# Second feed-forward in pairs of steps, its rank-2 additions in four groups of 32 rows, w13's low parts made by VectorE

## What is computed

```python
def attn(x, w_gate, w_up, w_down):           # I = 2752
    s = silu(x @ w_gate.T)
    s = s with its k = I/2 smallest |s| of each token set to 0
    return (s * (x @ w_up.T)) @ w_down.T

def qlora_linear(x, wq, A, B):               # wq is a quarter as wide; A, B have rank 2
    return x @ tile(wq, (1, 4)).T + (x @ A.T @ B.T) * 0.5

def ffn(x):
    return qlora(silu(qlora(x, w1q, a1, b1)) * qlora(x, w3q, a3, b3), w2q, a2, b2)

x = layernorm(x + attn(x)); x = layernorm(x + ffn(x))
```

## Time and profile before

| | us |
|---|---|
| median of 3 runs (2041.89 to 2043.99) | 2042.1 |
| the profiled execution's own time | 2044.99 |
| its span, first to last instruction | 2043.2 |
| PE busy in the span | 2001.4 |
| POOL busy | 1094.4 |
| DVE busy | 1110.7 |
| ACT busy | 799.2 |

### The profile page before, as it was taken

The page is one execution under the profiler, slowest core; times in us unless marked ns, Lnnn a source line. Parts: engine busy times, 40 slices in busy tenths (PEclk is TensorE's granted clock), DMA queues, the critical chain, the costliest instruction groups (busy, mean ns, idle before and its releaser), DMA issues.

```text
span 2043.2 us, 26001 instructions
## 1 busy us (share of the span) xinstructions
PE 2001.4 (98%) x9472; PEld 1635.8 (80%) x9472; DVE 1110.7 (54%) x1650; ACT 799.2 (39%) x1336; POOL 1094.4 (54%) x828
## 2 busy tenths in 40 slices
PE   8999999999999999999999999999979999999998
PEld 6887878888888888888888888887767777777776
DVE  0148984589763248976433888650145353454543
ACT  3357343562334347332333642422325325153251
POOL 6446984355546444644644455445738447175381
PEclk9999999999999999999999999999999999999999
DMA  4333333233434332433433243434422405124031
GB/s 139 97 92 86 116 102 92 83 114 118 135 88 126 97 94 93 139 119 104 125 97 94 93 138 96 133 94 154 137 78 93 144 21 174 42 90 146 21 133 42
DMA packets 104173, 213.40 MB, mean 104 GB/s; under 512 B 11896, under 2 KB 18040, under 8 KB 103012
## 3 DMA queue, kind: packets, MB, share of 16 engines
q1 hardware_dynamic: 99440, 194.97, 31.1%
q10 hardware_dynamic: 4608, 16.78, 2.1%
HBM read 194.93 MB, written 16.78 MB: 104 GB/s over the span
## 4 chain that ended last, share of the span: by engine, by line
PE 78%; issue 8%; POOL 8%; ACT 3%; DVE 2%; DMA 1%; SPq 0%; POOLq 0%; DVEq 0%; ACTq 0%
PE bank L1278 25%; PE bank L1279 24%; PE bank L1280 24%; POOL w13l L489 3%; POOL h2l L577 2%; PE bank L1316 2%; ACT junka L669 2%; POOL wl L489 1%; DMA w_in_place<-in_wd 1%; PE bank L1471 1%; PE bank L1433 1%; POOL xTl L489 1%; POOL hql L583 1%; PE bank L1424 0%; ACT wh L620 0%
## 5 line engine op out<-in xcount | busy, mean ns | idle before, releaser
L489 POOL TENSOR_TENSOR wl<-w_in_place,wh 128x512 fp32r<-128x512 f32 (+2 forms) x528 | 719.0, 1365 | 659.0 <-ACT wh L620 658.1
L620 ACT CAST wh<-w_in_place 128x512 fp32r<-128x512 f32 (+2 forms) x528 | 322.5, 612 | 774.8 <-DMA w_in_place<-in_wu 293.1
L1278 PE MATMUL bank<-wh,xTh 128*128 128x512 f32 (+1 forms) x1536 | 573.2, 373 | 13.2 <-POOL wl L489 13.2
L1280 PE MATMUL bank<-wh,xTl 128*128 128x512 f32 (+1 forms) x1536 | 570.1, 371 | 0.0
L1279 PE MATMUL bank<-wl,xTh 128*128 128x512 f32 (+1 forms) x1536 | 569.8, 371 | 0.0
L1278 PEld LDWEIGHTS bank<-wh,xTh 128*128 128x128 f32 x1536 | 290.4, 189 | 66.8 <-POOL wl L489 9.6
L1280 PEld LDWEIGHTS bank<-wh,xTl 128*128 128x128 f32 x1536 | 290.3, 189 | 50.7
L1279 PEld LDWEIGHTS bank<-wl,xTh 128*128 128x128 f32 x1536 | 290.5, 189 | 49.7
L1278 PE MATMUL bank<-wh,hTh 128*128 128x512 f32 (+1 forms) x704 | 274.6, 390 | 2.5 <-POOL wl L489 2.3
L1279 PE MATMUL bank<-wl,hTh 128*128 128x512 f32 (+1 forms) x704 | 274.1, 389 | 0.0
L1280 PE MATMUL bank<-wh,hTl 128*128 128x512 f32 (+1 forms) x704 | 273.9, 389 | 0.0
(11 more groups left out here) (132 smaller groups left out, 2456.3 us busy)
## 6 DMA issues: line engine op xcount, KB each, us to landing
w_in_place<-in_wg SPq DMA_DIRECT2D x160, 256.0 KB, 2.6
w_in_place<-in_wu SPq DMA_DIRECT2D x160, 256.0 KB, 2.6
w_in_place<-in_wd SPq DMA_DIRECT2D x160, 256.0 KB, 2.6
w_in_place<-in_w SPq DMA_DIRECT2D x90, 256.0 KB, 3.8
x_in_place<-in_xT SPq DMA_DIRECT2D x32, 256.0 KB, 3.5
y<-in_xtok SPq DMA_DIRECT2D x4, 2048.0 KB, 8.9
x<-y ACTq DMA_DIRECT2D x16, 512.0 KB, 4.1
xa<-x SPq DMA_DIRECT2D x16, 512.0 KB, 5.9
```

The costliest lines, as they stand in the source:

```text
L489: nc.gpsimd.tensor_tensor(lo, landed, hi.bitcast(F32), ALU.subtract).then_inc(done, 1)
L620: nc.scalar.copy(hi, piece).then_inc(hi_done, 1)
L1278: nc.tensor.matmul(dst, ah, bh, start=start, stop=False)
L1280: return nc.tensor.matmul(dst, al, bh, start=False, stop=stop)
```

## The change

- **Steps go in pairs.** PE makes the 24 large matmuls of two steps, then the four rank-2 additions of both, then the four `low_h` matmuls of the pair before. Gate and up of the pair's first step go to banks 0 and 1, of its second to banks 2 and 3, as before.
- **The additions use 6 rows each**, at rows 0, 32, 64 and 96 of `b13` and `lx`: one group of rows for each (gate, up) x (first, second step). `b13`, `lx` and `a13s` are laid out so (LX = 102 rows); `lg`, `lu`, `th`, `tl` are gone. `low_rank` now gives 102 rows, with each row of a1 and a3 repeated; DVE makes `lx` in three operations.
- **w13's low parts** of chunks 1 to 5 are made by DVE, in step q after the fold; those of chunk 0 stay with POOL. PE waits for `rest_lo`.
- **ACT** makes two high parts, two SiLUs, then the fold's high part and two `h2h`. **POOL** makes the fold's low part, then two `h2l`.
- **The down product's first tile** goes over chunks 0 to 4 for both halves before the last `low_h` and chunk 5.
- **Set-up**: POOL fills two masks with 36 small memsets in place of two selects and two of the zeroings; SP loads 18 small pieces of b in place of 12; DVE has one more pass over `b13`.

```diff
 # PE
-                for m in range(STEPS):
-                    c, q, rows = place(m)
+                for m0 in range(0, STEPS, 2):
+                    c, q, rows = place(m0)
                     if q == 0:
-                        pe.wait_ge(lo_done, base + 4 * c + 4)
+                        if c:
+                            pe.wait_ge(rest_lo, 4 * (CQ - 1) * b + 4 * c)
+                        else:
+                            pe.wait_ge(first_lo, 4 * b + 4)
                         pe.sem_inc(passed_pe, 1)
...
+                    for m in (m0, m0 + 1):
...
+                        for i in range(2):
+                            dst = banks[2 * (m - m0) + i][0:rows, :]
+                            if m >= 2:
+                                pe.wait_ge((s_done, h_done)[i], STEPS * b + m - 1)
+                                pe.sem_inc(passed_pe, 1)
+                            for k in range(KQ):
...
+                                three(dst, w13h[:, s, mm], w13l[:, s, mm], xsh[:, k, :], xsl[:, k, :], k == 0, False)
-                        nc.tensor.matmul(dst, b13[0:LR, mm], low_x[0:LR, :], start=False, stop=True).then_inc(done, 1)
-                    if m >= 2:
-                        low_h(b, m - 2, q == steps_of(c) - 1)
-                low_h(b, STEPS - 2, False)
+                    for m in (m0, m0 + 1):
+                        mm = slice(c * Q4 * P + place(m)[1] * rows, c * Q4 * P + (place(m)[1] + 1) * rows)
+                        for i, done in enumerate((gg_done, uu_done)):
+                            p0 = QUAD[2 * (m - m0) + i]
+                            nc.tensor.matmul(banks[2 * (m - m0) + i][0:rows, :], b13[p0:p0 + 3 * R, mm],
+                                             lx[p0:p0 + 3 * R, :], start=False, stop=True).then_inc(done, 1)
+                    if m0:
+                        low_h(b, m0 - 2, q + 2 == steps_of(c))
+                        low_h(b, m0 - 1, False)
...
-                    ins = nc.tensor.matmul(banks[7][0:2 * R, t * P:(t + 1) * P], a13s[:, k, :], x1T[:, k, :],
+                    ins = nc.tensor.matmul(banks[7][0:LX, t * P:(t + 1) * P], a13s[:, k, :], x1T[:, k, :],
 # PE, down_2, tile 0
+                    pe.wait_ge(h_done, STEPS * b + STEPS - 1)
...
+                    for n in range(2):
+                        for c in range(CQ - 1):
+                            add(n, c)
+                        if n == 0 and between is not None:
+                            between()
+                    low_h(b, STEPS - 2, False)
+                    low_h(b, STEPS - 1, False)
+                    pe.wait_ge(ql_done, CQ * (b + 1))
+                    pe.sem_inc(passed_pe, 1)
+                    for n in range(2):
+                        add(n, CQ - 1)
 # DVE
+            def low_13(b, c, i):
+                s, m = (c % 2) * 4 + i, steps_of(c) * rows_of(c)
+                dve.wait_ge(hi_done, USED2 + NW13 * b + 4 * c + i + 1)
+                V.tensor_tensor(w13l[:, s, 0:m], w13_in_place[:, s, 0:m], w13h[:, s, 0:m].bitcast(F32), ALU.subtract)\
+                    .then_inc(rest_lo, 1)
...
                     elif ins is not None:
                         step(ins)
+                    if c < CQ - 1:
+                        low_13(b, c + 1, q)
                     if 1 <= m <= NT:
                         norm_sums(NB + b - 1, [m - 1])
...
+                step(V.tensor_copy(lx[0:LX, :], banks[7][0:LX, :]))
+                step(V.tensor_scalar(rest[0:LX, :], banks[7][0:LX, :], split_x[0:LX, 0:1], None, ALU.mult))
                 st.done()
...
+                step(V.scalar_tensor_tensor(out=lx[0:LX, :], in0=lx[0:LX, :].bitcast(F32), scalar=split_x[0:LX, 1:2],
+                                            in1=rest[0:LX, :], op0=ALU.mult, op1=ALU.add))
 # ACT
+                for m in range(0, STEPS, 2):
+                    c, q, rows = place(m)
+                    if c < CQ - 1:
+                        high_13(b, c + 1, q)
+                        high_13(b, c + 1, q + 1)
+                    silu(m)
+                    silu(m + 1)
                     if q == 0 and c:
                         high_q(c - 1)
+                    high_h(m)
+                    high_h(m + 1)
...
 # POOL
-                for m in range(STEPS):
+                for m in range(0, STEPS, 2):
                     c, q, _ = place(m)
-                    if c < CQ - 1:
-                        low_13(b, c + 1, q)
-                    if m:
-                        low_h(m - 1)
                     if q == 0 and c:
                         low_q(c - 1)
+                    low_h(m)
+                    low_h(m + 1)
...
+                    for part, new, old, n in ((split_b, (LORA, -1.0), (0.0, 1.0), 2 * R), (split_x, (1.0, -1.0), (0.0, 1.0), R)):
+                        for i in range(2):
+                            fill(part[:, i:i + 1], old[i])
+                            for p0 in QUAD:
+                                fill(part[p0:p0 + n + R, i:i + 1], new[i])
+                                fill(part[p0:p0 + n, i:i + 1], old[i])
 # SP
-                    for i, (src, c0) in enumerate(((b1, 0), (b3, 0), (b2, IB), (b2, IB))):
+                    for i, src in enumerate((b1, b3, b1, b3)):
+                        r0 = UP * i + R * g
+                        sp.dma_start(braw[r0:r0 + R, 0:IB], src).then_inc(b_in, 16)
```

More of the change, by code:

```diff
@@ L70 @@
 LR = 96
+UP = 32
+QUAD = (0, UP, 2 * UP, 3 * UP)
+LX = QUAD[-1] + 3 * R
 NW2, NW13 = 2 * CQ, 4 * CQ
@@ L566, in _, with low_13 @@
                     less(w2h[0:rows, c, sl], w2l[0:rows, c, sl], w2_in_place[0:rows, c, sl], w2_lo)
-            def low_13(b, c, i):
-                s, m = (c % 2) * 4 + i, steps_of(c) * rows_of(c)
-                low(USED2 + NW13 * b + 4 * c + i, w13h[:, s, 0:m], w13l[:, s, 0:m], w13_in_place[:, s, 0:m])
+            def low_13(b, i):
+                m = steps_of(0) * rows_of(0)
+                pool.wait_ge(hi_done, USED2 + NW13 * b + i + 1)
+                less(w13h[:, i, 0:m], w13l[:, i, 0:m], w13_in_place[:, i, 0:m], first_lo)
             def steps_2(b, last):
@@ L819, in high_q, with silu @@
                     nc.scalar.copy(hqh[0:rows, c, :], fold[0:rows, :]).then_inc(qh_done, 1)
[L821 to L824 removed]
+                def silu(m):
+                    rows = place(m)[2]
                     act.wait_ge(gg_done, STEPS * b + m + 1)
@@ L1472, in steps_2 @@
-                    if m >= 2:
-                        low_h(b, m - 2, q == steps_of(c) - 1)
-                low_h(b, STEPS - 2, False)
-            def down_2(b, t, between=None):
+                    for m in (m0, m0 + 1):
+                        if m < 2 and b:
+                            pe.wait_ge(e_evac, 2 * NT * b - 2 + 2 * m)
+                            pe.sem_inc(passed_pe, 1)
+                        for i in range(2):
+                            dst = banks[2 * (m - m0) + i][0:rows, :]
[3 more added lines that the diff above has]
+                            for k in range(KQ):
+                                s, mm = (c % 2) * 4 + 2 * i + k, slice(place(m)[1] * rows, (place(m)[1] + 1) * rows)
+                                three(dst, w13h[:, s, mm], w13l[:, s, mm], xsh[:, k, :], xsl[:, k, :], k == 0, False)
@@ L1478, in down_2, with add @@
+            def down_2(b, t, between=None):
+                tt = slice(t * P, (t + 1) * P)
+                def add(n, c):
+                    rows, w = rows_of(c), slice(n * 512, (n + 1) * 512)
+                    three(banks[2 * (t % 2) + n][:, :], hqh[0:rows, c, tt], hql[0:rows, c, tt], w2h[0:rows, c, w],
+                          w2l[0:rows, c, w], c == 0, False)
                 if t == 0:
+                    pe.wait_ge(h_done, STEPS * b + STEPS - 1)
+                    pe.sem_inc(passed_pe, 1)
@@ L1479, in down_2 @@
                     pe.wait_ge(ql_done, CQ * b + CQ - 1)
                     pe.sem_inc(passed_pe, 1)
-                elif t >= 2:
-                    pe.wait_ge(e_evac, 2 * NT * b + 2 * (t - 1))
-                    pe.sem_inc(passed_pe, 1)
[L1484 to L1496, removed]
+                    for n in range(2):
[3 more added lines that the diff above has]
+                            between()
@@ new lines, in down_2 @@
+                    low_h(b, STEPS - 2, False)
+                    low_h(b, STEPS - 1, False)
+                    pe.wait_ge(ql_done, CQ * (b + 1))
+                    pe.sem_inc(passed_pe, 1)
+                    for n in range(2):
+                        add(n, CQ - 1)
+                else:
+                    if t >= 2:
+                        pe.wait_ge(e_evac, 2 * NT * b + 2 * (t - 1))
+                        pe.sem_inc(passed_pe, 1)
+                    for n in range(2):
+                        for c in range(CQ):
+                            add(n, c)
+                        if n == 0 and between is not None:
+                            between()
@@ L1581 @@
         w2[CQ - 1, at:at + LASTQ] = w2t[(CQ - 1) * P:]
```

(5 more changed lines are left out.)

87 lines of the change are left out of this document (31 added, 56 removed).

## The result

The changed kernel takes 2184.7 us (median of 4 runs, 2180.8 to 2187.8) against 2043.1 us: ratio 1.069, 95% interval 1.068 to 1.070. Forecast were 2222 us in a range of 2148 to 2262: the sign and the mechanism were right, the added time was forecast 38 us too large.

A forecast was written before the change was run, and what follows sets the result against it. PE, busy 98% of the span, was taken as the bound. Terms: additions -14, chunk waits +134, clock +44, low_rank +8, down turn +8, pair turns +5, replaced waits -3, set-up -2: +180 on 2042.1, 2222 us; range 2148 to 2262.

The forecast's parts named there:

- the sign: Whole kernel: the change makes it slower than before, chance 0.96; faster 0.03, within 0.2% 0.01.
- the mechanism: Second feed-forward, chunks 1 to 5: PE waits for DVE's low parts queued behind h and fold, +134 us; lower clock afterwards, +44.
- the added time: Whole kernel: all terms together add +180 us to the runs' median of 2042.1 us.

## What to carry to other kernels

When work moves to another engine, ask first behind what it is queued there: with the same 80 subtractions on DVE the kernel takes 154 us more when they stand behind h than when they stand ahead of it, because their inputs do not depend on the pair's additions, while h waits for these. Batching steps moves all their follow-up work behind one point, so whatever PE needs at the next turn must be made before that point. And a pause can cost more than its length: here the clock after it added a third (36 us on 115).

## What the runs showed of the hardware

- Four K=6 matmuls of 512 columns at rows 0, 32, 64 and 96, into four banks, cost 0.53 us together, where four over the whole array take 0.93; 0.09 of the 0.53 us is the way in, and going back to the whole array shows no gap.
- Pauses of PE of 4.8 to 7.0 us were followed by the lower clock level every time (20 of 20); pauses of 1.7 to 2.5 us three times of 20, each time after one of the longest.
- A weight load of 102 columns shows 176 ns in a row against 87 for 4 columns, and still 16 passes with the wide load take 1.66 us from first start to the next matmul's, 0.10 each, against 1.84 with the narrow one: the length of a load in a row is not its slot.
- An operation of DVE that waits for nothing started 0.61 us after the start of a 0.69 us one, so 0.08 us decided which of two two-input operations of DVE and POOL ran at its own length (0.68 us for DVE) and which was stretched (1.72 us for POOL, 1.29 alone).
